# Second layer norm's Newton step moved from VectorE to GpSimd in a fused metaformer kernel

## The reference, cut to what matters

```python
def _ln_c(v, eps=1e-06):                 # first norm, over the channels of a pixel
    m = jnp.mean(v, axis=1, keepdims=True)
    s = jnp.var(v, axis=1, keepdims=True)
    return (v - m) / jnp.sqrt(s + eps)

def _ln_t(v, eps=1e-05):                 # second norm, over the channels of a token
    m = jnp.mean(v, axis=-1, keepdims=True)
    s = jnp.var(v, axis=-1, keepdims=True)
    return (v - m) / jnp.sqrt(s + eps)

x = x + conv(_ln_c(x))                   # group norm, two 1x1 convolutions with a relu between, residual
t = _to_tokens(x)                        # 16384 tokens of 64 channels a batch
t = t + ffn(_ln_t(t))                    # 32 experts each pick their 8 best tokens
```

## Time and profile before

| | |
|---|---|
| median of 3 runs | 632.74 us (632.73 to 635.37) |
| profiled execution: its own time | 639.6 us |
| profiled execution: span on the core | 637.9 us |
| TensorE busy | 535.4 us (84%) |
| VectorE busy | 487.2 us (76%) |
| ScalarE busy | 435.3 us (68%) |
| GpSimd busy | 189.6 us (30%) |
| granted TensorE clock, mean of the span | 0.935 |

### The profile page before, as it was taken

One profiled execution on the slowest core, in us unless ns is written; L12 is line 12 of the kernel. 1 busy time (PEld: TensorE's weight loads), 2 busy tenths in 40 slices (PEclk: granted clock), 3 DMA queues, 4 the chain that ended last, 5 costly groups with the idle time before them and its releaser, 6 DMA issues.

```text
span 637.9 us, 14170 instructions
## 1 busy us (share of the span) xinstructions
PE 535.4 (84%) x5732; PEld 270.3 (42%) x5732; DVE 487.2 (76%) x950; ACT 435.3 (68%) x651; POOL 189.6 (30%) x116
## 2 busy tenths in 40 slices
PE   2749999898998899889989899989887988876982
PEld 1324444444444344444444444444443433434762
DVE  5574556689888988898789878988888687799620
ACT  2463779677976797679767976797677855984110
POOL 1007435023502260217020802080207145121144
PEclk9955999999999999999999999999998998987595
DMA  8960144714471447244634454445401255430000
GB/s 195 195 144 0 68 133 142 188 68 133 133 199 67 134 133 191 76 133 134 168 98 134 115 160 123 133 101 165 133 35 67 76 182 154 146 100 5 6 15 19
DMA packets 26752, 73.38 MB, mean 115 GB/s; under 512 B 4152, under 2 KB 4152, under 8 KB 22592
## 3 DMA queue, kind: packets, MB, share of 16 engines
q1 hardware_dynamic: 25664, 71.44, 40.9%
q0 software_dynamic: 1024, 1.05, 0.6%
HBM read 38.40 MB, written 34.08 MB: 114 GB/s over the span
## 4 chain that ended last, share of the span: by engine, by line
PE 41%; DVE 30%; ACT 13%; issue 12%; DMA 2%; POOL 1%; SPq 0%; ACTq 0%; DVEq 0%; POOLq 0%
PE st L372 11%; ACT junk L801 7%; DVE xs L948 7%; PE cv L383 6%; PE cv L391 6%; PE tl L400 6%; PE bc L494 5%; DVE us L938 5%; DVE lg L936 3%; DVE top_i L1035 2%; ACT tok L766 2%; DVE us L940 2%; DVE cnd L1030 2%; DMA xs<-in_x 2%; PE tl L409 2%
## 5 line engine op out<-in xcount | busy, mean ns | idle before, releaser
L1426 POOL TENSOR_TENSOR xs<-xs,us 128x1024 f32<-128x1024 f32 x64 | 151.2, 2379 | 367.2 <-DVE xs L948 173.4
L948 DVE SCALAR_TENSOR_TENSOR xs<-cv,vecs,xs 128x1024 f32<-128x1024 f32 x64 | 82.1, 1282 | 47.8 <-PE cv L391 47.7
L794 ACT ACTIVATE sqc<-us 128x1024 f32<-128x1024 f32 x64 | 67.5, 1054 | 46.2 <-DVE us L938 45.4
L761 ACT ACTIVATE hid<-cv,b1n 128x1024 f32<-128x1024 f32 x64 | 71.2, 1113 | 36.5 <-PE cv L383 36.0
L938 DVE TENSOR_TENSOR us<-xs,bc 128x1024 f32<-128x1024 f32 x60 | 73.0, 1216 | 19.7 <-PE bc L494 19.3
L400 PEld LDWEIGHTS tl<-ident,xs 128*128 128x128 f32 x512 | 63.8, 195 | 53.9 <-issue 53.9
L372 PE MATMUL st<-xs,stat_w 128*32 128x256 f32 x1024 | 74.5, 413 | 10.5 <-DMA xs<-in_x 9.4
L801 ACT ACTIVATE junk<-us 128x1024 bf16<-128x1024 f32 x64 | 67.3, 1051 | 22.8 <-DVE gsum L940 22.1
L940 DVE CUSTOM_DVE_ANT_0 us<-us,bc 128x1024 f32<-128x1024 f32 x60 | 72.9, 1215 | 11.2 <-PE bc L494 9.9
L400 PE MATMUL tl<-ident,xs 128*128 128x128 f32 x512 | 76.4, 294 | 0.9 <-ACT lg L776 0.9
L409 PE MATMUL tl<-xs,gcen 128*32 128x256 f32 x1024 | 69.4, 389 | 8.0 <-ACT tok L766 7.9
(11 more groups left out here) (210 smaller groups left out, 652.4 us busy)
## 6 DMA issues: line engine op xcount, KB each, us to landing
xs<-in_x SPq DMA_DIRECT2D x64, 512.0 KB, 7.0
out_rows<-tok SPq DMA_DIRECT2D x64, 512.0 KB
us<-in_e_w SPq DMA_DIRECT2D x8, 260.0 KB
xs<-in_e_w SPq DMA_DIRECT2D x8, 256.0 KB
sqc<-out_rows,idx_all POOLq DMA_INDIRECT x16
out_rows<-sqc,idx_all POOLq DMA_INDIRECT x16, 2.1
vecs<-in_b SPq DMA_DIRECT2D x4, 0.2 KB, 14.0
gate_bias<-in_gate_b SPq DMA_DIRECT2D x4, 0.1 KB, 12.3
```

Source lines behind the costliest of these rows:

```text
L948: nc.vector.scalar_tensor_tensor(out=xu, in0=cv[:], scalar=vecs[:, 3:4], in1=xu, op0=ALU.add, op1=ALU.add).then_inc(x1_done, 1)
L1426: nc.gpsimd.tensor_tensor(xu, xu, su, ALU.add).then_inc(s_done, 1)
```

## The change

The four operations of the Newton step of the second norm go to GpSimd for batches 0 to 6. VectorE had done them in three instructions, since its two-operation form does a scalar and a tensor operation at once; on GpSimd they are `v2*y2`, `*y2`, `*(-0.5) + 1.5` and `*y2`, each of 256 columns, each waiting for the one before. They stand in GpSimd's list between the additions of units 5 and 6 of the batch. VectorE waits for their result and keeps the two instructions that round and split it. Batch 7 stays on VectorE as a whole.

```diff
             def ln2_rstd(f):
                 link = ln2
-                dve.wait_ge(y2_ready, f + 1)
-                newton(link, v2[:], y2[:], tb[:], 0.0)
-                link(nc.vector.scalar_tensor_tensor(out=tb[:], in0=tb[:], scalar=1.5, in1=y2[:], op0=ALU.add, op1=ALU.mult))
+                if f < NB - 1:
+                    dve.wait_ge(root2_ready, f + 1)
+                else:
+                    dve.wait_ge(y2_ready, f + 1)
+                    newton(link, v2[:], y2[:], tb[:], 0.0)
+                    link(nc.vector.scalar_tensor_tensor(out=tb[:], in0=tb[:], scalar=1.5, in1=y2[:], op0=ALU.add, op1=ALU.mult))
                 link(nc.vector.tensor_copy(hi[:], tb[:]))
                 nc.vector.scalar_tensor_tensor(out=rstd2_s[:], in0=hi[:].bitcast(F32), scalar=second[:], in1=tb[:],
                                                op0=ALU.mult, op1=ALU.add).then_inc(rstd2_ready, 1)
...
             pool.wait_ge(const_p, 2)
+            def root2(f):
+
+                pool.wait_ge(y2_ready, f + 1)
+                cp(nc.gpsimd.tensor_tensor(tb[:], v2[:], y2[:], ALU.mult))
+                cp(nc.gpsimd.tensor_tensor(tb[:], tb[:], y2[:], ALU.mult))
+                cp(nc.gpsimd.tensor_scalar(tb[:], tb[:], -0.5, 1.5, ALU.mult, ALU.add))
+                nc.gpsimd.tensor_tensor(tb[:], tb[:], y2[:], ALU.mult).then_inc(root2_ready, 1)
+
             for n in range(NB):
                 for k in range(NU):
+                    if k == LATE_ADDS[0] and n > 0:
+                        root2(n - 1)
                     add(n, k)
```

More of the change, by code:

```diff
@@ L233, in mk_metaformer_kernel @@
         msq_done, var2_ready, ln2_done, y2_ready = (sem(n) for n in ("msq_done", "var2_ready", "ln2_done", "y2_ready"))
-        ln2_steps, rstd2_ready = sem("ln2_steps"), sem("rstd2_ready")
+        ln2_steps, rstd2_ready, root2_ready = sem("ln2_steps"), sem("rstd2_ready"), sem("root2_ready")
         top_steps, top_ready, expl_done, cnd4_ready = (sem(n) for n in ("top_steps", "top_ready", "expl_done", "cnd4_ready"))
@@ L1022, in ln2_rstd @@
                                                op0=ALU.mult, op1=ALU.add).then_inc(rstd2_ready, 1)
-                assert link.n == LN2_STEPS * (f + 1), link.n
+                assert link.n == 2 * (f + 1) + 3 * max(0, f + 2 - NB), link.n
             def top_values(t, i):
```

## The result

The changed kernel takes 636.2 us (median of 15 runs, 635.43 to 638.04); the kernel before, in 15 runs with it, 633.73 us (632.67 to 635.37). The ratio is 1.0045, with a 95% interval of 1.0033 to 1.0056. It is slower by 0.45%, some 2.5 to 3 us, which is within 0.5% but clear of the noise. 631.6 us was forecast, with a range up to 634.2: wrong side, and outside.

The account below looks back on a forecast made before the run. No engine is full; TensorE, VectorE and ScalarE hand work to each other in a chain. -2.5 us in rounds 2 to 6, 0 in round 1, +1.42 us in round 7 make -1.1 us: 632.74 to 631.6, range 630.1 to 634.2.

Parts of the forecast that it names:

- The chain on GpSimd: The four Newton operations on GpSimd were to take 2.65 us, between 2.28 and 3.44 us.
- Rival (a): GpSimd's chain too slow, before VectorE's cast: break-even about 3.5 us, at 4.0 us the kernel takes 636.3; chance 0.10.
- Rounds 2 to 6: VectorE's cast comes 1.35 us earlier, but `x1` waits for `conv2`: 0.50 us won a round, 2.5 us in five.
- rival (d): In rounds 2 to 6 `conv2` itself comes earlier, up to 1.35 us a round: 627.4 us; chance 0.05.
- Round 1: `x1` is already bound by `conv2`, so nothing won or lost, 0.2 us lost at the upper bound.
- Round 7: No cover: VectorE's cast waits for GpSimd and comes 1.42 us later, lost in full.
- rival (c): Round 7's delay is absorbed by another chain later in it or in the tail: -2.5 us, 630.2; chance 0.10.
- rival (b): VectorE and GpSimd block each other at line 1098 in rounds 2 to 6: up to +1.4 us, 634.1; chance 0.12.
- the sum: Terms from full-clock rounds add to -1.1 us, put unchanged on the runs' median of 632.74: 631.6 us.

Follow-up runs that it names:

- r7_alone_pool: The kernel before with only batch 6's Newton step (round 7) moved to GpSimd; ratio 1.0042 to the kernel before.
- no_step_r1_6: The changed kernel with the Newton step left out for batches 0 to 5 and batch 6 on VectorE; ratio 0.9972 to the kernel before.
- after_every_filled: The changed kernel with products of zeros in TensorE's waits in rounds 0 to 6 and 12 more in round 7's wait; ratio 0.9989 to the kernel before.
- after_all_filled: The changed kernel with products of zeros in TensorE's waits in rounds 0 to 6, none in round 7's; ratio 0.9991 to the kernel before.
- before_again: The kernel before, unedited, run for a second trace; ratio 1.0006.
- r7_on_vector: The changed kernel with batch 6's Newton step (round 7) back on VectorE, batches 0 to 5 on GpSimd; ratio 0.9984 to the kernel before.
- before_all_filled: The kernel before with products of zeros ahead of five waiting spreads a round and in round 6's waits; ratio 0.9976 to the kernel before.

## Why the prediction was wrong

**The chain on GpSimd** was sized well: 0.73 us a product for 0.67, 0.41 for 0.46, 0.08 us between them for 0.06; 2.85 us for 2.65. Rival (a) is out: the kernel is slower, but not by a slow chain. The estimate by the figure of the Trainium skill (GPSIMD Engine Reference, section 3.1), 0.79 us a product, was 8% over.

**Rounds 2 to 6**: right, and a little better than forecast. 0.60 us a round and not 0.50: 0.53 us at `x1` of unit 1 (9.01 to 8.48) and 0.06 us at the next. The wait of `x1` for `conv2` appeared as forecast, and rival (d), 1.35 us a round, is out. Round 1 neither won nor lost (8.48 us to `x1` of unit 1 in both).

**Round 7**: the wait was right, 1.45 us by the milestones for 1.42 us forecast, and nothing took it up before the last `x1`; r7_alone_pool is 0.42% slower. So rival (c) is out. "Lost in full" was too little: the slow clock behind the wait came on top.

**Blocking between the engines**, rival (b): no_step_r1_6, without any chain, had the same rounds, so it is out for this place. Line 1101 took 0.17 us as without the chain, but that says little: it started in the last 0.07 us of an operation of GpSimd (252.81 - 252.74). The case that the prediction priced, a VectorE instruction held by a whole one on GpSimd, did not come up.

**The step that failed** is in the sum: "the terms come from rounds at full clock, so I put the same difference on the median of the runs". With that the change's effect on the clock was a term of nothing, without a reason. The terms themselves were right at full clock: after_every_filled shows their sum up to the last `x1`, -1.36 us against -1.1 us. In the kernel as it is they do not come at full clock. Against a kernel before without a drop in its rounds, the traces have:

- -3.0 us in five rounds and +1.45 us of waiting in round 7, the terms that were forecast (at -2.5 and +1.42 us)
- +1.5 us for the drop that each of three traces of the changed kernel has in step 3
- +0.6 us for the longer slow stretch in round 6
- +0.65 us for the half clock behind round 7's wait (1.54 us in r7_alone_pool, 2.12 us in after_all_filled)

These make +1.2 us, where 2.5 to 3 us were measured. The three terms of clock, 2.75 us, are shown: the products of zeros take them away in rounds 0 to 6 and behind round 7's wait. The other 1.3 to 1.8 us are not shown. The tail could hold them, as it took 78.9 us in two traces of the changed kernel and 77.5 us in before_again, but it took 78.6, 78.5 and 78.4 us in three other traces with VectorE's round 7.

Two ratios over many runs say the same in the large: six batches on GpSimd won 1.0 us and not 3.0 (r7_on_vector), and the seventh cost 2.7 us and not 1.4 (r7_alone_pool). The mean granted clock, on record for every run, agrees: 0.924 to 0.928 in the 15 runs of the changed kernel, and a median of 0.933 to 0.935 in the runs of the kernel before beside the experiments.

My prediction read the waits of 0.8 to 2 us on TensorE as idle time that costs nothing, and took the change as neutral to them. Round 6 of the trace of before had the warning in it, 1.72 and 1.97 us where 1.09 and 1.16 are usual, behind a wait of 1.83 us.

**What stays open.** The tail took 77.2 to 80.7 us for the same work, at a granted clock of 0.66 to 0.72. It was 78.3 us and more in five of the six traces with round 7 on GpSimd and in three of the eight others. Round 7 from `x1` of unit 1 and the tail together took 118.8 to 120.8 us in the six, and 117.5 to 118.6 us in seven of the eight (121.8 us in the first trace of before, with its unexplained wait). So something behind that `x1` is lost with round 7 on GpSimd, part of it in the slow stretch and part in the tail. That the delay of 1.45 us moves the tail's own waits to a worse place is a guess that no run tested. Nor is it settled how often the kernel before has a drop in executions without a trace: its two traces have none and one. And what decides which of two waits of the same length loses the clock is not known: that its place in time does is theory B, and the runs show only that products in the wait keep the clock.

The kernel with batches 0 to 5 on GpSimd, batch 6 on VectorE, and products of zeros in the waits beats both: 631.19 us in the median of 12 runs, ratio 0.9957 (0.994 to 0.9974). Against the kernel before with the same products, 632.38 us, the 1.2 us are not clear of the noise.

## What to carry to other kernels

A term of 0.5 us a round worked out at full clock is no more certain than the clock, if TensorE waits about a microsecond several times a round: look up how many slow stretches the trace has, and behind which waits, before summing. Move work off an engine only where its result is covered, round by round: here six batches had 2 us of cover or more and the seventh had none, and its wait alone cost half of what five rounds won. And take milestones from two or three traces of the same kernel before reading a difference of a few microseconds from one.

## What the runs showed of the hardware that was not expected

The granted clock of TensorE fell to half (from 1.00 to 0.50) behind waits as short as 0.83 us, with one of 0.90 us shortly before, and stayed behind others of 1.20 us; the same wait in the same kernel did one or the other from round to round and from trace to trace. A drop cost 1.5 us in most cases and up to 2.9 us. In before_all_filled 6 to 8 small products ahead of five waiting spreads of a round kept the clock full from 66 to 514 us, at a cost of 0.1 us a round (65.3 us for 65.2) and 0.4 us in round 0.

The time to `x1` of unit 1 of round 0, in identical code, was 62.05 us in one trace of the kernel before and 66.19 us in another.
